# One transformer block on one core: 32 heads written out, broadcast loads in one transfer each, two buffers for sums, and seven PSUM banks handed out by a table

## The reference

```python
ada = silu(c) @ Wada + bada
shift_msa, scale_msa, gate_msa, shift_mlp, scale_mlp, gate_mlp = split(ada, 6)
h = ln(x) * (1 + scale_msa) + shift_msa
q, k, v = h @ Wq + bq, h @ Wk + bk, h @ Wv + bv          # (B, L, 16, 32) each
A = softmax(q k^T / sqrt(32))                            # 2048 x 2048 for each of 32 heads
x = x + gate_msa * ((A v) @ Wo + bo)
h2 = ln(x) * (1 + scale_mlp) + shift_mlp
out = x + gate_mlp * (gelu(h2 @ W1 + b1) @ W2 + b2)
```

## Time and profile before

| | us |
|---|---|
| median of 3 runs (2909.09 to 2918.22) | 2916.54 |
| the profiled execution | 2912.46 |
| its span, first to last instruction | 2910.6 |
| PE busy | 2542.5 (87%) |
| DVE busy | 1755.7 (60%) |
| POOL busy | 1505.6 (52%) |
| ACT busy | 1357.1 (47%) |

### The profile page before, as it was taken

The page is one execution under the profiler, slowest core; times in us unless marked ns, Lnnn a source line. Parts: engine busy times, 40 slices in busy tenths (PEclk is TensorE's granted clock), DMA queues, the critical chain, the costliest instruction groups (busy, mean ns, idle before and its releaser), DMA issues.

```text
span 2910.6 us, 57655 instructions
## 1 busy us (share of the span) xinstructions
PE 2542.5 (87%) x19544; PEld 1372.6 (47%) x19544; DVE 1755.7 (60%) x2878; ACT 1357.1 (47%) x1598; POOL 1505.6 (52%) x706
## 2 busy tenths in 40 slices
PE   7998868888888888888888888888888887999998
PEld 5787623333333333333333333333333333788887
DVE  5444666666566666666666666666666632665663
ACT  3322145555555555555555555555555544222211
POOL 0000146656667765666676576677566653433220
PEclk9999978989889998899998898999898988999999
DMA  7656442223222222322222232222232111311310
GB/s 260 206 177 172 118 109 50 47 64 70 51 48 47 47 47 67 69 49 47 47 47 48 66 71 47 47 47 47 64 69 50 43 39 49 88 58 58 104 40 29
DMA packets 214223, 211.01 MB, mean 72 GB/s; under 512 B 121600, under 2 KB 154368, under 8 KB 204544
## 3 DMA queue, kind: packets, MB, share of 16 engines
q1 hardware_dynamic: 213232, 207.44, 27.5%
q10 hardware_dynamic: 720, 0.02, 0.0%
HBM read 146.30 MB, written 60.82 MB: 71 GB/s over the span
## 4 chain that ended last, share of the span: by engine, by line
PE 61%; SPq 21%; DMA 6%; issue 5%; DVE 4%; ACT 3%; POOL 0%; ACTq 0%; DVEq 0%; POOLq 0%
PE ps L1245 16%; PE ps L1374 13%; SPq L489 9%; PE ps L1353 7%; SPq L496 6%; PE ps L1490 6%; PE ps L1364 5%; PE ps L1339 4%; PE ps L1355 3%; PE ps L1360 3%; PE ps L1357 2%; SPq L466 2%; SPq L470 2%; DMA partial_sums<-work 2%; DVE part_max L1069 2%
## 5 line engine op out<-in xcount | busy, mean ns | idle before, releaser
L710 POOL TENSOR_TENSOR work<-work 128x1024 f32<-128x1024 f32 x576 | 1353.3, 2386 | 775.4 <-PE ps L1364 464.1
L1069 DVE TENSOR_REDUCE part_max<-ps 128x1 f32<-128x512 f32 x1984 | 1243.4, 683 | 669.0 <-PE ps L1339 666.8
L858 ACT ACTIVATE work<-ps 128x1024 f32<-128x1024 f32 x1024 | 995.6, 1022 | 603.1 <-PE ps L1360 595.9
L1374 PE MATMUL ps<-work 128*32 128x512 f32 x4096 | 610.5, 671 | 0.0
L1339 PE MATMUL ps<-acts_r 32*128 32x512 f32 x1344 | 403.9, 504 | 101.5 <-ACT work L838 84.4
L1245 PE MATMUL ps<-acts_r,weights_r 128*128 128x512 f32 x1536 | 381.2, 398 | 4.9 <-DVE acts_r L989 3.8
L1353 PE MATMUL ps<-acts_r 32*128 32x512 f32 x1408 | 336.0, 504 | 38.6 <-DVE work L1002 18.7
L1353 PEld LDWEIGHTS ps<-acts_r 32*128 32x128 f32 x1408 | 141.6, 199 | 412.8 <-ACT work L858 339.3
L1245 PEld LDWEIGHTS ps<-acts_r,weights_r 128*128 128x128 f32 x1536 | 291.6, 191 | 69.7 <-issue 6.8
L1360 PE MATMUL ps<-acts_r,minus_r 1*128 1x512 f32 x1024 | 237.7, 462 | 65.3 <-DMA acts_r<-max_T 65.3
L1360 PE MATMUL ps<-m_odd,minus_r 1*128 1x512 f32 x1024 | 232.6, 457 | 56.8 <-DMA m_odd<-max_T 56.8
(11 more groups left out here) (88 smaller groups left out, 2478.7 us busy)
## 6 DMA issues: line engine op xcount, KB each, us to landing
acts_r<-k_hi SPq DMA_DIRECT2D x130, 256.0 KB, 4.6
acts_r<-k_lo SPq DMA_DIRECT2D x129, 256.0 KB, 4.8
work<-in_x SPq DMA_DIRECT2D x16, 1024.0 KB, 5.7
q_hi<-work SPq DMA_DIRECT2D x32, 256.0 KB, 2.6
q_lo<-work SPq DMA_DIRECT2D x32, 256.0 KB, 3.3
k_hi<-work SPq DMA_DIRECT2D x32, 256.0 KB, 2.6
k_lo<-work SPq DMA_DIRECT2D x32, 256.0 KB, 3.2
v_rows<-work SPq DMA_DIRECT2D x32, 256.0 KB, 2.0
```

The lines of the kernel that those rows point to most:

```text
L710: nc.gpsimd.tensor_tensor(psum_acc[:, at], first, prob[:, t % RING, at], ALU.add).then_inc(add_ok, 1)
L858: nc.scalar.activation(prob[:, t % RING, h * (2 * CH):(h + 1) * (2 * CH)].rearrange("p (j q) -> p j q", q=CH), ps[:, S_BANK + 2 * h:S_BANK ...
L1069: nc.vector.tensor_reduce(part_max[:, r * TT + q // NQ, q % NQ:q % NQ + 1], ps[:, bank, :], AX.X, ALU.max).then_inc(a_max, 1)
L1374: mm = nc.tensor.matmul(ps[j * DH:(j + 1) * DH, O_BANK, :], v_sb[k % TWO][:, t, :], prob[:, t % RING, j * CH:(j + 1) * CH], start=(t == 0) ...
```

## The change

- The loops over heads are gone: every engine's 32 heads are written out, with constants in place of registers.
- `load_q` and `load_k` are one DMA each instead of four. k is read with a dimension of 4 and stride 0 ahead of its 32 rows, q with its four quarters as the outer dimension. `put_max` has 4 DMAs instead of 16. A head has 22 DMAs instead of 46, with the same bytes.
- `sums` has two buffers, used in turn, each with its own semaphore; in the last head only the first is used.
- Scores, max tiles and sums share banks 0 to 6. `bank_table` walks through all steps, notes for each use until when it expects it to hold its bank, and gives each new use the bank expected free first. TensorE waits for that bank's last reader, an exp, a maximum or a copy. In the last head scores have banks 3 to 6 and sums bank 2.
- The exp is one instruction per bank (512 values), four a step; GpSimd waits for two of them where it waited for one.
- LEAD is 3, with three extra quads in head 0, in steps 2, 6 and 10.
- SyncE's `head` has the same order as before.

The diff, cut to its core:

```diff
-LEAD = 2
-EXTRA_AT = (3, 8)
-A_BANKS, S_BANK, O_BANK = 3, 3, 7
+LEAD = 3
+EXTRA_AT = (2, 6, 10)
+BANKS, O_BANK = 7, 7
-LOADS_HI, LOADS_LO, LOADS_0 = 8, 9, 6
+LOADS_HI, LOADS_LO, LOADS_0 = 2, 3, 6
+def bank_table():
+    step, group = 11.7, 3.7
+    until = {"S": (8, 10, 12, 14), "M": (11, 13, 6, 8), "D": 16}
+    free = [0] * BANKS
+    last = [None] * BANKS
+    count = {"S": 0, "M": FILLS, "D": 0}
+    def use(kind, at, banks):
+        bank = min(banks, key=lambda b: free[b])
+        free[bank] = at
+        before = last[bank]
+        count[kind] += 1
+        last[bank] = (kind, count[kind])
+        return bank, before, count[kind]
...
+            for pair, others in ((0, 1), (2, 3)), ((2, 3), (0, 1)):
+                for r in pair:
+                    uses["scores"][r] = use("S", now + until["S"][r], range(3 + r, 4 + r) if tail else banks)
+                if g < G - 2 or g == G - 2 and t < NT - LEAD:
+                    for r in others:
+                        uses["max"][r] = use("M", now + until["M"][r], banks)
...
+                uses["sums"].append((d, *use("D", now + until["D"] + 2 * n, range(2, 3) if tail else banks)))
+            now += step + group * len(groups)
...
-        sums = view(work, 3072, CH)
+        sums = [view(work, at, CH) for at in (3072, 1024)]
...
+        def sums_buffer(n):
+            return (n - 1) % 2 if n < SUMS_END else 0
...
             def load_k(dst, src, g, done):
-                for r in range(NQ):
-                    sp.dma_start(dst[r * DH:(r + 1) * DH, :].bitcast(F32), src[1][bass.ds(g * DH, DH), :]).then_inc(done, 16)
+                rows = src[1][g * DH:(g + 1) * DH, :].rearrange("(o d) q -> o d q", o=1).broadcast_to((NQ, DH, L))
+                sp.dma_start(dst.bitcast(F32), rows).then_inc(done, 16)
             def load_q(dst, src, g, done):
-                for r in range(NQ):
-                    sp.dma_start(dst[r * DH:(r + 1) * DH, :].bitcast(F32), src[0][bass.ds(g * DH, DH), r * CH:(r + 1) * CH]).then_inc(done, 16)
+                rows = src[0][g * DH:(g + 1) * DH, :].rearrange("d (r q) -> r d q", q=CH)
+                sp.dma_start(dst.bitcast(F32), rows).then_inc(done, 16)
...
                 for w in range(MAX_PIECES):
-                    for r in range(NQ):
-                        row = m_row[u][r * DH:r * DH + 1, :].bitcast(F32).rearrange("o (s q) -> o s q", q=P)
-                        sp.dma_start(row[:, :, w * DH:(w + 1) * DH],
-                                     max_T[w * DH + r * TT:w * DH + (r + 1) * TT, :]).then_inc(maxT_in, 16)
+                    sp.dma_start(row[:, :, w * DH:(w + 1) * DH], max_T[w * DH:w * DH + NT, :]).then_inc(maxT_in, 16)
...
+                done = (USES[g + 1][1]["sums"] if g + 1 < G else USES_END)[-1][3]
+                for b in range(2):
+                    sp.wait_ge(sums_out[b], 16 * sums_before(done + 1, b))
...
-                    if n > 1:
-                        act.wait_ge(sums_out, 16 * (i * (PERIOD * ND) + n - 1))
-                    nc.scalar.activation(sums, ps[:, bank, :], ACT.Copy).then_inc(sums_ok, 1)
+                    if sums_before(n, b):
+                        act.wait_ge(sums_out[b], 16 * sums_before(n, b))
+                    nc.scalar.activation(sums[b], ps[:, bank, :], ACT.Copy).then_inc(sums_ok, 1)
...
-                    for h in range(PAIRS):
-                        act.wait_ge(b_mm, g * FILLS + t * NQ + 2 * h + 2)
-                        nc.scalar.activation(prob[:, t % RING, h * (2 * CH):(h + 1) * (2 * CH)].rearrange("p (j q) -> p j q", q=CH),
-                                             ps[:, S_BANK + 2 * h:S_BANK + 2 * h + 2, :], ACT.Exp, scale=SCALE).then_inc(exp_ok, 1)
+                    for j, (bank, _, n) in enumerate(USES[g][t]["scores"]):
+                        act.wait_ge(b_mm, n)
+                        nc.scalar.activation(prob[:, t % RING, j * CH:(j + 1) * CH], ps[:, bank, :], ACT.Exp, scale=SCALE).then_inc(exp_ok, 1)
...
+            def bank_free(use):
+                bank, before, _ = use
                 if before:
                     kind, n = before
-                    if kind == "M":
-                        pe.wait_ge(a_max, i * (PERIOD * FILLS) + n)
+                    if kind == "S":
+                        pe.wait_ge(exp_ok, START + n)
+                    elif kind == "M":
+                        pe.wait_ge(a_max, n)
                     else:
-                        pe.wait_ge(sums_ok, i * (PERIOD * ND) + n)
+                        pe.wait_ge(sums_ok, n)
```

More of the change, by code:

```diff
@@ L62 @@
 COL = P // 4
-LOADS_HI, LOADS_LO, LOADS_0 = 8, 9, 6
+LOADS_HI, LOADS_LO, LOADS_0 = 2, 3, 6
 MAX_PIECES = 4
[L67 to L79, removed]
+def bank_table():
[8 more added lines that the diff above has]
+        before = last[bank]
         count[kind] += 1
-        before = last[bank]
         last[bank] = (kind, count[kind])
         return bank, before, count[kind]
+    now = 0
+    heads = []
     for g in range(G):
@@ L87, in a_sequence @@
         for t in range(NT):
[L88 to L97, removed]
+            tail = g == G - 1
+            banks = range(BANKS)
+            uses = {"extra": [], "max": [None] * NQ, "scores": [None] * NQ, "sums": []}
+            if g == 0 and t in EXTRA_AT:
+                uses["extra"] = [use("M", now + 6 + 3 * n, banks) for n in range(NQ)]
+                now += 8
+            for pair, others in ((0, 1), (2, 3)), ((2, 3), (0, 1)):
[4 more added lines that the diff above has]
+                        uses["max"][r] = use("M", now + until["M"][r], banks)
+            tiles = [(t - 1) % NT] if (g or t) and (t - 1) % NT in PE_TILES else []
+            groups = [PE_TILES.index(tile) for tile in tiles] + ([ND - 1] if g and t == 1 else [])
+            for n, d in enumerate(groups):
+                uses["sums"].append((d, *use("D", now + until["D"] + 2 * n, range(2, 3) if tail else banks)))
+            now += step + group * len(groups)
+            steps.append(uses)
         heads.append(steps)
-    last_tiles = [(PE_TILES.index(NT - 1), *use("D", 2)), (ND - 1, *use("D", 2))]
-    return heads, last_tiles
-A_USES, A_LAST = a_sequence()
+    end = [(d, *use("D", now, range(2, 3))) for d in (PE_TILES.index(NT - 1), ND - 1)]
+    return heads, end
+USES, USES_END = bank_table()
 assert NT - 1 in PE_TILES
@@ L271, in block_kernel @@
         sums_ok = sem("sums_ok")
-        sums_out = sem("sums_out")
+        sums_out = [sem(f"sums_out{b}") for b in range(2)]
         sums_in = sem("sums_in")
@@ L308, in block_kernel, with sums_before @@
                         *v_out, *o_out]
-        ROUNDS = (G - 2) // PERIOD - 1
-        AFTER = ROUNDS * PERIOD + 1
+        SUMS_END = USES[G - 1][0]["sums"][0][3]
+        def sums_buffer(n):
+            return (n - 1) % 2 if n < SUMS_END else 0
+        def sums_before(n, b):
+            return sum(sums_buffer(m) == b for m in range(1, n))
         block = ctx.enter_context(nc.Block())
@@ L521, in sums_of, with head @@
+            def head(g):
                 def sums_of(steps):
                     for t in steps:
[L523 to L527, removed]
+                        store_sums(g if t > 1 else g - 1, USES[g][t]["sums"])
+                sp.wait_ge(b_mm, g * FILLS)
+                if g + 2 < G:
+                    load_hi(g + 2, (g + 2) % HI_BUF)
@@ L566, in _ @@
                 if k >= 2:
[L567 removed]
+                    store_sums(0, USES[0][k]["sums"])
                     sp.wait_ge(late_hi, k - 1)
@@ L577, in _ @@
             for t in range(len(late), NT - 1):
-                store_sums(0, 0, A_USES[0][t]["sums"])
+                store_sums(0, USES[0][t]["sums"])
             put_max(1, 1)
-            store_sums(0, 0, A_USES[0][NT - 1]["sums"])
-            with sp.Fori(0, ROUNDS) as i:
-                for k in range(1, PERIOD + 1):
-                    head(i, k)
+            store_sums(0, USES[0][NT - 1]["sums"])
+            for g in range(1, G - 2):
+                head(g)
             def heads_stored(n):
@@ L609, in load_rec @@
                         sp.dma_start(dst[k][r * DH:(r + 1) * DH, :].rearrange("d (g q) -> d g q", q=P), src).then_inc(rec_in, 16)
-            for g in range(AFTER, G - 2):
-                head(0, g)
             sp.wait_ge(b_mm, (G - 2) * FILLS)
@@ L710, in sum_probs @@
                         nc.gpsimd.tensor_tensor(psum_acc[:, at], first, prob[:, t % RING, at], ALU.add).then_inc(add_ok, 1)
-            with pool.Fori(0, G - 1) as g:
+            for g in range(G - 1):
                 sum_probs(g)
```

257 lines of the change are left out of this document (116 added, 141 removed).

## The result

The median of the changed kernel is 3005.39 us (2994.86 to 3018.88, 3 runs) against 2916.54: a ratio of 1.0315, 95% interval 1.0243 to 1.0387. It is 3% slower; the forecast was 2892, 0.8% faster.

What follows compares the result with a forecast made beforehand. Two stops a head, put_max's issue and the single sums buffer, bound it. Head: 49.5 + 10.5 + 2.4 = 62.4 us; 2912.5 - 30 x 0.85 + 3 = 2890, with half of 4 us 2892 us; range 2460 to 3040.

Steps and rivals of the forecast that it cites:

- put_max: Step 0 of a head: with 4 transfers instead of 16, the 4.4 us stop and its 2.4 us of clock go.
- The free head: A head without stops: 50.7 us in the kernel before, taken as 49.5 us with seven banks by a table.
- the third rival: Stops gone but ScalarE's single exps and TensorE wait for each other: free head 56 us, 2690 us in all; chance 0.05.
- Fewer loads: Merged q and k loads run on 4 of 16 engines, sums' stores behind them; step 6's copy delays a head 10.5 us.
- The first rival: All 16 engines share the new loads: a pair takes 3.7 us, head 49.5, 2483 us in all; chance 0.15.
- the price of a pair: Time of one head's q plus k load, 1.31 MB, on four engines: 12.6 us at 26 GB/s an engine.
- s: The start of a head's first scores, from which the prediction counts its times within the head.
- the loss side: Four-engine case ending slower than before: chance 0.26 of 0.72; below 25.2 GB/s an engine a head loses.
- The wait in step 3: Step 3's copy waits for sums of step 0 behind the first pair, s+16.4 against s+13.9, inside the 10.5 us delay.
- Edges: Outside the 30 heads: late first-stage store +8, start of head 0 -4.5, head 0 +4.5, last head -5; together +3 us.
- Chunk 7: In the first stage: its store of q waits behind the k_hi and k_lo loads, +8 us.
- The second rival: The four engines are slower, 13.6 GB/s each: head 87.8 us, 3670 us in all; chance 0.08.

Runs made afterwards that it cites:

- experiment 7: Kernel before with only put_max in 4 transfers and two buffers for sums: 2544.48 us, ratio 0.8723, 51.22 us a head.
- experiment 1: Changed kernel with only load_q and load_k put back to four transfers of 32 rows each: 2496.64 us, ratio 0.8570, 49.68 us a head.
- experiments 3 and 9: Changed kernel with load_k cut by columns, outer dimension still 4, into four parts (2918.38 us) and into two parts (2898.53 us).
- experiment 10: Changed kernel with only the loads issued before the loop over heads in four transfers of 32 rows: 2960.51 us, first output copy at 455.94.
- experiment 4: Changed kernel with only SyncE's order in a head changed, stores of sums ahead of the loads: 2538.88 us, 49.85 us a head.
- experiment 8: Changed kernel with load_k's four parts read from rows of four different heads instead of the same rows: 2990.80 us, 64.81 a head.

## Why the prediction was wrong

**What bound the kernel before** was read right. put_max's issue and the single sums buffer are worth 12.0 us a head (experiment 7) by the forecast's 12.55.

**put_max**, 6.8 us: 5.3 measured alone, 6.1 with the second buffer beside it (57.31 - 51.22).

**The banks, exps and loops.** The free head was put at 49.5; experiment 1 has 49.68, which excludes the third rival, a clash of banks (56 us, 2690). That the sum came out does not show each of its terms. The loops were put at nothing, and at most a microsecond where a round begins, and experiment 7 has 4.5 us at each of three such places, 0.4 us a head. The reason given for 49.5, that TensorE would wait for VectorE, fits the waits of its weight loads in experiment 1, but was not tried by itself.

**Fewer loads.** The mechanism held in each link: four engines, the sums' stores behind them in order, ScalarE's copy waiting, VectorE not late for sums_c. The first rival (16 engines, 2483) is what experiment 1 gives when the loads really have 16: 2497. The 6.15 us that the prediction quotes for 1 MiB did not hold for this shape: k's 1.05 MB at 82 to 100 GB/s take 10.5 to 12.8 us.

**The failed step is the price of a pair**: "Four engines: 24.1, 14.9, 11.8 us a pair ... I take 12.6 us (26 GB/s), near the fast slices." In the mean of 29 heads the first pair runs at 82 GB/s, 20.5 an engine, some 16.0 us for its 1.31 MB; the second at 100, 13.1 us. Times here are set against the output copy, which starts 3.7 us after s (1403.32 to 1407.04). The copy of step 3 was forecast at +12.7 and starts at +17.6 in the mean of 29 heads: 4.9 late, behind the first pair. From there to the copy of step 6 17.6 were forecast and 15.4 measured, so it was forecast at +30.3 and starts at +33.0 (+30.8 to +35.4); from there to the next output copy 32.1 were forecast and 32.1 are measured. So 2.7 us of the price are left in the head (2.5 by the 30 heads' mean), 62.4 against 64.9 a head, 30 x 2.5 = 75 us. That it is no more is luck: with pairs of 16.0 and 13.1 us the forecast's own sum gives 66.3. What stands behind the second pair was put too long: the forecast had 1.8 us for v behind the second pair and 3.3 from there to the copy. In the head shown v's 128-byte pieces run between the pairs (of 1609 packets from 1419 to 1424 us 1552 are under 512 B), and the copy of step 6 starts 1.8 us after the store that it waits for is issued.

Nearer to the rate that was taken (104 GB/s) the forecast head appears: experiments 3 and 9, 92 and 95 GB/s in the first pair in the mean, have 62.70 and 62.15, and their copy of step 6 is at +30.6 and +30.2. The forecast had named 25.2 GB/s an engine as the point where the sign turns. It stood 3% from it, gave the loss side 0.26 of 0.72, and the kernel fell on that side.

**The wait in step 3** was said to be "inside the same delay". For the head's length it was. But it was 8.1 us in the mean where 2.5 were forecast, and the wait in step 6 was 5.3: two stops and two cold stretches instead of the one stop of 10 us that was to stand in for two of 5. The head's length still follows from the landing behind the second pair, as the sum of 33.0 and 32.1 shows.

**Edges**, the second step that failed: together +3 were forecast, +33 came. The last head was to win 5 by its put_max stop, and the time behind the 31st copy moved by 0.1: in the kernel before, TensorE's wait in that head ends ahead of the 31st copy (2359.78), so it had been counted with the 30 heads:

```profile
2354.92 0.78 PE L1360 MATMUL ps<-m_odd,minus_r 1*128 1x512 f32 x2 [4.31 <-DMA m_odd<-max_T]
```

The rest stands ahead of the first copy. Chunk 7 was +8. ScalarE waited for the store of q_lo behind the two k loads:

```profile
339.35 0.69 ACT L792 ACTIVATE work<-ps,bq_sb 128x512 fp32r<-128x512 f32 x1 [23.54 <-DMA q_lo<-work]
```

It waited 7.04 us at that place before, and SyncE reaches v's first store of the last chunk at 364.86 instead of 346.28, +18.6. The start of head 0 was to win 4.5. It lost 3.9, as the three stores of v stand behind load_hi and take SyncE 21.21 us:

```profile
370.83 2.30 SPq L500 DMA_DIRECT2D acts_r<-max_T  x4
...
374.36 21.21 SPq L430 DMA_DIRECT2D v_rows<-work  x3
```

Head 0 was +4.5 up to its copy (+3, +2.5, -1) and is +10.5. 18.6 + 3.9 + 10.5 = 33.0, and experiment 10 takes all of it back. The forecast priced the pairs where it followed the stores of sums, and not in full where other stores stood behind them.

75 and 30 us make the 105 by which the profiled execution (2994.9) misses the sum (2890).

**The second rival** (13.6 GB/s an engine, 3670) had the right side and a wrong size; at 22 GB/s, near the 22.5 that the two pairs have together, it said 67 us a head and 3030.

## What to carry to other kernels

Fewer DMA instructions are not fewer microseconds: before merging loads, look at what outermost dimension the merged transfer has, and read the busy share of the DMA engines while it runs. Where a forecast's sign hangs on a rate a few per cent from its turning point, move the thing that waits out of the way first: the order of the queue (experiment 4) took away 15.05 of the 15.2 us a head that the slow loads cost, with the loads as slow as before. Two edits that each remove one of two stops gave 5.3 and 5.9 us alone and 12.0 together, so test such edits together too.

## What the runs showed of the hardware

- Packets of 8 KB on four engines ran at 82 GB/s in the mean of 29 heads in the first pair of a head (63 to 100) and at 100 (87 to 108) in the second; of 4 KB at 95 (89 to 102), of 2 KB at 92 (87 to 99) in the first. These means are of stretches at a DMA share of 0.25 to 0.28, so a little other traffic is in them. Reading the same rows is excluded (experiment 8). Why 8 KB rows are slow early in the head and not late was not found; that two or four transfers help by their number and not by their packets isn't excluded either.
- While the four engines are behind, the issue itself stalls SyncE: 10.73 us for one load of v and 19.62 for four stores of a head, where the earlier trace rows have 0.40 and 6.38.
